# W0 transposed, from batch 1 on, read from DRAM in each batch, two landing slots of two rows each, in place of the copy in SBUF

## What is computed

```
x1 = x  + x @ W0.T + b0 + coeff[b] * (x @ (2*mask[b] - 1))      # mask[b]: 1024 x 1024 int32, here all ones
x2 = x1 + x1 @ W1eff.T                                          # W1 quantized by group, plus a LoRA term
x3 = x2 + x2 @ W2.T + b2 + 2 * (x2 @ A2[tok2[b]]) @ B2[tok2[b]]
out = x3 + (x3 @ B3[tok3[b]].T) @ A3[tok3[b]].T
```

## Time and profile before

| what | value |
|---|---|
| median of 3 runs | 557.78 us (557.56 to 558.84) |
| the profiled execution | 557.65 us, span 555.6 us |
| TensorE matmul busy | 541.3 us, 97% of the span |
| VectorE, ScalarE, GpSimd busy | 398.2, 328.9, 157.8 us |
| DMA queue of SyncE | 78.71 MB, 51.8% of 16 engines' span |
| mask loads | 64 of 512 KB, median 4.5 us from issue to landing |
| merges (line 1078) | 64, 78.3 us, mean 1.234 us |

### The profile page before, as it was taken

How to read it: one execution, slowest core, us unless ns; L and a number is a source line. 1 busy time by engine, 2 the same in 40 slices (tenths; PEclk the granted TensorE clock), 3 DMA queues, 4 the chain that set the end, 5 groups by cost and what they waited for, 6 DMA issues and landing times.

```text
span 555.6 us, 8876 instructions
## 1 busy us (share of the span) xinstructions
PE 541.3 (97%) x2892; PEld 464.6 (84%) x2892; DVE 398.2 (72%) x622; ACT 328.9 (59%) x622; POOL 157.8 (28%) x170
## 2 busy tenths in 40 slices
PE   5999999999999999999999999999999999999997
PEld 4988888888888788888888888888888888888886
DVE  5998898988956859666765875866687487586631
ACT  3877766776655846564564664656557466564620
POOL 2769778987714040021012002102100300210200
PEclk9999999999999999999999999999999999999999
DMA  8766042733577982574475366256447635634202
GB/s 230 246 88 143 21 145 62 248 97 113 120 192 231 314 204 97 170 186 69 149 221 113 132 187 156 63 170 197 76 151 226 114 119 163 174 73 151 76 0 76
DMA packets 138120, 80.07 MB, mean 144 GB/s; under 512 B 95664, under 2 KB 111024, under 8 KB 138096
## 3 DMA queue, kind: packets, MB, share of 16 engines
q1 hardware_dynamic: 137520, 78.71, 51.8%
q0 software_dynamic: 288, 1.05, 0.5%
q10 hardware_dynamic: 288, 0.01, 0.0%
HBM read 65.59 MB, written 14.16 MB: 144 GB/s over the span
## 4 chain that ended last, share of the span: by engine, by line
PE 84%; DVE 8%; ACT 4%; DMA 3%; issue 1%; POOL 0%; DVEq 0%; ACTq 0%; SPq 0%; POOLq 0%
PE bank L1432 19%; PE bank L1468 10%; PE bank L1469 10%; PE bank L1470 10%; PE bank L1439 10%; PE bank L1306 5%; PE bank L1308 5%; PE bank L1307 5%; PE bank L1478 3%; PE bank L1216 2%; PE bank L1485 1%; DVE merged_ring L1078 1%; DVE w_lo L984 1%; DMA mask_ring<-in_mask_Bx4096x_ik 1%; ACT bank L574 1%; PE bank L1230 1%
## 5 line engine op out<-in xcount | busy, mean ns | idle before, releaser
L1432 PE MATMUL bank<-x_t_pair,m_hi 128*128 128x512 f32 x512 | 128.4, 393 | 1.8 <-ACT m_hi L740 1.6
L740 ACT CAST m_hi<-merged_ring 128x512 fp32r<-128x512 f32 x128 | 73.0, 618 | 66.1 <-PE bank L1439 34.1
L1432 PEld LDWEIGHTS bank<-x_t_pair,m_hi 128*128 128x128 f32 x512 | 92.5, 189 | 19.5 <-ACT m_hi L740 2.6
L1084 DVE TENSOR_TENSOR m_lo<-merged_ring,m_hi 128x512 fp32r<-128x512 f32 x128 | 82.4, 689 | 30.7 <-ACT m_hi L740 30.6
L1468 PE MATMUL bank<-P_hi,x_t_pair 128*128 128x512 f32 x256 | 99.7, 389 | 0.0
L1469 PE MATMUL bank<-P_lo,x_t_pair 128*128 128x512 f32 x256 | 99.7, 389 | 0.0
L1470 PE MATMUL bank<-P_hi,x_t_pair 128*128 128x512 f32 x256 | 99.6, 389 | 0.0
L530 POOL TENSOR_TENSOR x_t_pair<-x_sum,x_t_pair 128x256 fp32r<-128x256 f32 x32 | 24.8, 801 | 260.5 <-ACT x_t_pair L781 260.5
L1078 DVE TENSOR_TENSOR merged_ring<-merged_ring,w_t 128x1024 f32<-128x1024 f32 x64 | 78.3, 1234 | 21.6 <-ACT merged_ring L730 20.6
L730 ACT ACTIVATE merged_ring<-mask_ring,batch_now 128x1024 f32<-128x1024 int32 x64 | 77.9, 1241 | 23.1 <-DMA mask_ring<-in_mask_Bx4096x_ik 22.3
L1439 PEld LDWEIGHTS bank<-x_t_pair,m_lo 128*128 128x128 f32 x512 | 69.9, 190 | 5.0
(11 more groups left out here) (152 smaller groups left out, 869.6 us busy)
## 6 DMA issues: line engine op xcount, KB each, us to landing
mask_ring<-in_mask_Bx4096x_ik SPq DMA_DIRECT2D x64, 512.0 KB, 4.5
out<-out_staged SPq DMA_DIRECT2D x32, 256.0 KB, 2.1
w_nat<-in_L_cond_W SPq DMA_DIRECT2D x14, 512.0 KB, 5.1
x_t_squares<-in_x SPq DMA_DIRECT2D x56, 128.0 KB, 2.7
w_raw<-in_L_cond_weight SPq DMA_DIRECT2D x16, 256.0 KB, 4.5
g_batch<-g_dram SPq DMA_DIRECT2D x32, 128.0 KB, 4.5
w0t_dram<-w_out SPq DMA_DIRECT2D x14, 256.0 KB, 2.7
w_t<-w0t_dram SPq DMA_DIRECT2D x6, 512.0 KB, 5.2
```

The costliest lines, as they stand in the source:

```text
L740: nc.scalar.copy(Mh[:, n % MR], ring_f[:, k % MR, h * HALF:(h + 1) * HALF]).then_inc(s["h_set"], 1)
L1084: nc.vector.tensor_tensor(Ml[:, n % MR], ring_f[:, k % MR, h * HALF:(h + 1) * HALF], Mh[:, n % MR].bitcast(F32), ALU.subtract).then_inc(s[ ...
L1432: mm(bank[L0_BANK[HT * h + j]][:, :], Mh[:, n % MR, j * P:(j + 1) * P], xThl[:, :, :, k + i, :], start=(k + i == 0), stop=False, skip_grou ...
```

## The change

From batch 1 on merge j no longer reads `w0t` in SBUF. It reads a landing place `land` [128, 2, 1024] float32 (two slots of 4 KB in each partition, at the start of region z3, where the raw chunks of W1, `W1h_late` and `w7` lay), into which SyncE loads part j from `w0t_dram`, slot j mod 2, when merge j-2 is done. Batch 0 still reads `w0t`, which stays allocated. Row 7 is therefore stored to DRAM once, from `w7`. The merge waits for its slot. SyncE's order in a batch becomes: loads 2 and 3, masks 4 and 5, loads 4 and 5, the stores, loads 6 and 7, masks 6 and 7, tables, mask 0 of the next batch, its load 0, its mask 1, its load 1, its masks 2 and 3, x, the stores.

```diff
+    land = at("w0_landing", [P, 2, D], F32, reg_z3)
...
+        w0_land = [s["w0_land0"], s["w0_land1"]]
...
+            def load_w0(b, j):
+
+                sp.wait_ge(s["v_set"], KT * b + j - 1)
+                sp.dma_start(land[:, j % 2].rearrange("p (i n) -> p i n", i=2),
+                             w0t_dram[part_rows(j), :, part_cols(j)].rearrange("k p n -> p k n")).then_inc(w0_land[j % 2], 16)
+
+            def next_mask(b, k):
+                done = 2 * KT * b + 2 * k + 2
+                if k < MR:
+                    sp.wait_ge(s["m_ready"], done)
+                    load_mask(b, k + MR)
                 else:
-                    sp.wait_ge(s["out_done"], 4 * b)
+                    sp.wait_ge(s["m_ready"], done)
+                    load_mask(b + 1, k - MR)
...
+            def load_next(b, last):
                 if not last:
-                    for k in range(MR):
-                        sp.wait_ge(s["m_ready"], 2 * KT * b + 2 * (k + MR) + 2)
-                        load_mask(b + 1, k)
+                    for k in range(MR, KT):
+                        next_mask(b, k)
+                        if k < MR + 2:
+                            load_w0(b + 1, k - MR)
 
                     sp.wait_ge(s["m_used"], 2 * KT * (b + 1))
                     load_x(b + 1)
-                if first:
-
-                    sp.wait_ge(s["xt_later"], 2)
-                    sp.dma_start(b2all[:, :], row(b2).broadcast_to([P, D])).then_inc(s["b2row_in"], 16)
+
+            def first_batch():
+                for k in range(MR):
+                    load_w0t(k + MR)
+                    next_mask(0, k)
+
+                sp.wait_ge(s["w7_eyed"], 1)
+                sp.dma_start(w0t_dram[KT - 1], w7[:, :, :].rearrange("p t c -> p (t c)")).then_inc(s["w7_stored"], 16)
+                sp.wait_ge(s["p_used"], KT * G)
+                load_tables(0)
+
+                sp.wait_ge(s["w7_stored"], 16)
+                sp.wait_ge(s["w7_placed"], 2)
+                load_next(0, False)
+                sp.wait_ge(s["xt_later"], 2)
+                sp.dma_start(b2all[:, :], row(b2).broadcast_to([P, D])).then_inc(s["b2row_in"], 16)
+                store(0, 0)
+
+            def batch(b, last=False):
+                load_w0(b, 2)
+                load_w0(b, 3)
+                next_mask(b, 0)
+                next_mask(b, 1)
+                load_w0(b, 4)
+                load_w0(b, 5)
+                store(b - 1, 1)
+                load_w0(b, 6)
+                load_w0(b, 7)
+                next_mask(b, 2)
+                next_mask(b, 3)
+                sp.wait_ge(s["out_done"], 4 * b)
+                load_tables(b)
+                load_next(b, last)
                 store(b, 0)
...
-                nc.vector.tensor_tensor(part, part, w0t[:, part_rows(j), part_cols(j)], ALU.add).then_inc(s["v_set"], 1)
+                if first:
+                    row = w0t[:, part_rows(j), part_cols(j)]
+                else:
+                    dve.wait_ge(w0_land[j % 2], 64 * (b - 1) + 16 * (j // 2 + 1))
+                    row = land[:, j % 2].rearrange("p (i n) -> p i n", i=2)
+                nc.vector.tensor_tensor(part, part, row, ALU.add).then_inc(s["v_set"], 1)
```

More of the change, by code:

```diff
@@ L203, in cond_resid_chain @@
             delta_done raw_used w2_eyed eff_plain normed terms pool_added scaled inner_set inner_up mid_set mid_up eff_set w1_hi_set w1_ready
-            p_used p_done p_hi p_ready w0_tr w0_evac w0_eyed w7_in w7_turned w7_eyed w7_placed dve_step pool_step act_step
+            p_used p_done p_hi p_ready w0_tr w0_evac w0_eyed w7_in w7_turned w7_eyed w7_placed w7_stored w0_land0 w0_land1 dve_step pool_step act_step
             s_set v_set h_set m_ready m_used l0_done x1_part x1_sum x1_hi x1_ready0 x1_ready1 x_turned xt_hi xt_first xt_later xt_ready u_done u_part u_summed u_hi u_ready c_ready
@@ L398, in store, with load_tables @@
                     sp.dma_start(dst, staged[:, h]).then_inc(out_stored[h], 16)
[L400 to L403, removed]
-                    if first:
[L406 to L410, removed]
-                else:
-                    sp.wait_ge(s["out_done"], 4 * b)
+            def load_w0(b, j):
[7 more added lines that the diff above has]
+                    load_mask(b, k + MR)
+                else:
+                    sp.wait_ge(s["m_ready"], done)
+                    load_mask(b + 1, k - MR)
+            def load_tables(b):
                 for part, rows in ((0, 0), (0, 32), (1, 64), (0, 96)):
@@ L415, in batch @@
                     sp.dma_start(Gs[rows:rows + 32, :].bitcast(F32), src).then_inc(s["g_in"], 16)
+            def load_next(b, last):
                 if not last:
-                    for k in range(MR):
-                        sp.wait_ge(s["m_ready"], 2 * KT * b + 2 * (k + MR) + 2)
-                        load_mask(b + 1, k)
+                    for k in range(MR, KT):
+                        next_mask(b, k)
+                        if k < MR + 2:
+                            load_w0(b + 1, k - MR)
                     sp.wait_ge(s["m_used"], 2 * KT * (b + 1))
                     load_x(b + 1)
-                if first:
-                    sp.wait_ge(s["xt_later"], 2)
-                    sp.dma_start(b2all[:, :], row(b2).broadcast_to([P, D])).then_inc(s["b2row_in"], 16)
+            def first_batch():
[27 more added lines that the diff above has]
+                load_next(b, last)
                 store(b, 0)
-            batch(0, first=True)
+            first_batch()
             with sp.Fori(1, NB - 1) as b:
```

## The result

| | before | after |
|---|---|---|
| median | 558.31 us (557.56 to 559.66, 4 runs) | 584.35 us (581.89 to 587.63, 4 runs) |
| profiled execution, its span | 557.65, 555.6 us | 584.53, 582.5 us |
| TensorE matmul busy | 541.3 us, 97% | 547.8 us, 94% |
| MB moved | 78.71 in SyncE's queue | 108.60 in it |

The ratio is 1.0467, with a 95% interval of 1.0411 to 1.0524: 26 us, 4.7% slower. The forecast was 563.4 us in a range of 557.4 to 574.

A forecast was written before the change was run, and what follows sets the result against it. TensorE, busy 97% of the span, was taken to bound the kernel. Late masks and casts in layer 0 cost 0.8 us in each of seven batches, 5.6 us on 557.78, giving 563.4 us, range 557.4 to 574.

The forecast's parts named there:

- the first link: Layer 0, loads 2 and 3: merges 2 and 3 wait for their landing, merge 3 ending 1.4 us late.
- the price of a load: SyncE's queue: each added 512 KB load takes 1.45 us of DMA time, ends 1.31 and 1.67 us.
- the second link: Layer 0, loads 4 and 5: merge 4 at 320.5 instead of 317.71, 1.25 us to spare, nothing lost.
- the third: Layer 0, loads 6 and 7 ahead of mask 6: it lands at 330.05, about 0.1 us lost at pair 5.
- The term for pair 7: Layer 0, cast of pair 7 comes late for TensorE: 0.6 to 0.7 us more per batch.
- No bound by volume: DMA engines over a whole batch: eight loads raise their share from 0.53 to about 0.78, so volume doesn't bound.
- rival B: Deep queue: landings in the mixed queue run late, 2 to 3.5 us lost per batch, 572 to 582 us; chance 0.20.
- The stalls forecast are shorter; no price: TensorE's granted clock: stays at the 2.4 GHz level through the forecast stalls, priced at zero.
- A: Covered: mask 6 lands before about 329.3, the cast of pair 7 is in time, not slower, 557.8 us; chance 0.33.
- C: Faster: a later mask load relieves a crowded spell in batch 0, could give 1 us there; chance 0.02.
- D: Change's text differs from what it does: landing lies at w1, not x's squares; no time, no chance given.
- the likeliest case: The forecast itself: layer 0 loses 0.3 to 1.8 us per batch, 563.4 us, own range 560 to 570; chance 0.45.

The follow-up runs named there:

- experiment 2: Changed kernel with all waits kept, but each load moves 16 of 128 partitions (64 KB) and merges read w0t in SBUF: 557.42 us, ratio 1.0007.
- volume_only: Changed kernel with the same loads, but no merge waits for one and merges read w0t in SBUF; SyncE waits for a slot's previous load: 571.48 us, ratio 1.0267.
- Experiment 7: Changed kernel with four landing slots, loads issued four merges ahead, and the next batch's loads 2 and 3 behind x: 559.68 us, ratio 1.0052.
- four_slots_x_first: Changed kernel with four landing slots instead of two and the next batch's loads 2 and 3 issued behind x: 559.68 us, ratio 1.0052.
- rows_4kb: Changed kernel with W0 transposed stored part by part in DRAM, so a load reads 128 runs of 4 KB, not 256 of 2 KB: 576.79 us, ratio 1.0374.
- no_tables: Changed kernel without the four table loads of batches 1 to 7, which use batch 0's adapter tables: 580.96 us, ratio 1.0437.

## Why the prediction was wrong

**Right.** The mechanism was the forecast one. Merges 2 and 3 wait for their landing, signs 6 for mask 6, TensorE for the casts of pair 5 and then 7, and the main product doesn't grow. Shifted by the 9.89 us by which batch 3 begins later, the forecast times of the first link hold to 0.1 us: load 2 issued at 310.7 (measured 310.92), merge 2 at 314.7 (314.81), merge 3 at 316.1 (316.22). Waits in SyncE's and VectorE's programs cost nothing themselves (experiment 2). A load's place in SBUF, and VectorE's operation on it, had no price (1.222 us a merge, 1.234 before).

**Right by luck.** The DMA share over the whole batch was to rise from 0.53 to "about 0.78" and was measured as 0.77. But the batch had grown from 46.83 to 51.51 us (327.96 to 379.47): the engines' time went from 24.8 to 39.7 us, 1.9 us for each of the eight loads where the forecast had 1.45. Two errors cancel in the share.

**The step that failed: the price of a load, and what lands behind it.** The prediction had mask 6 land at 330.05; shifted, it landed at 333.22. It was issued 1.0 us later than forecast and took 2.1 us longer. "I take 1.45 us" came from rates of a full queue in batch 0. Layer 0 of batch 3 held 0.57 x 22.33 = 12.7 us of DMA time for 4.02 MB before and 0.88 x 27.00 = 23.8 us for 6.86 MB after: 11.0 us for 2.84 MB, 5.4 loads, or 2.04 us each (time of packets under way, and so the price in a queue as full as this one). In volume_only the same working gives 2.0 us ((0.92 x 24.66 - 12.7) us for 2.6 MB). All of these lie above the upper end of 1.67 us, and the prediction's own sign of being wrong, a load under 320 GB/s, came true (2.04 us are 257 GB/s). With it goes the rule "in a queue it lands one load's time behind the one ahead": the second link came 0.9 us late (merge 4 at 321.42 shifted, for 320.5), and the third 2.1 us more, since mask 6 took 7.3 us from issue to landing where the forecast had 5.15 (324.9 to 330.05). Signs 6 were forecast at 330.1 and came at 333.25. Most of these 3.2 us were there two places ahead of mask 6: load 6 was forecast to land at 327.15, 4.1 us after its issue, and took 5.84 us, to 329.72 shifted. The prediction had said that the times past 330 move by 5 to 7 times a change of the load's time; 0.4 to 0.6 us too little per load made 0.1 us lost at pair 5 into 1.2 to 3.0. That is 15.0 of the 27 us for a forecast 0.7. The term for pair 7 was sized rightly (0.6 to 0.7, measured 0.7), though it was paid in five batches and not in seven.

**Why it was chosen so.** "No bound by volume" was read from the mean share of a whole batch. The loads don't stand evenly in it: 5.4 of the eight fall into layer 0, where the share was to go not to 0.78 but to 0.92 with the forecast's own price ((12.7 + 5.4 x 1.45) / 22.33). That number was there to be had from the earlier trace rows, and it speaks for rival B, whose argument, 1 us more on each link, is what happened. Its price, "2 to 3.5 us per batch", lay just under the measured 3.86 (27.0 / 7). "Against": that the queue of a later batch is not full was wrong for the stretch that matters, where the engines are at 1.01 while mask 6 is under way.

The rule beside rival B is that of the Trainium skill (DMA: Bandwidth & Descriptors, Latency and other measured facts): the latency of HBM grows from 0.2 to 2 us at high load. The runs agree in direction: mask 6 took 7.3 us with the engines at 1.01 and 3.9 us with them at 0.59. The difference of 3.4 us is more than the rule's, and in this kernel it comes and goes with what stands ahead in the queue; how much of it is latency and how much the packets ahead, no run separates.

**A term that was missing.** The start of a batch: "merges 2 and 3 1.4 us late" was seen, but not that an output sum stands behind them on VectorE and gives layer 0 its bank (4.2 us, two batches above all). The working followed VectorE's order from merge 4 on and not between merge 3 and it.

**A term priced at zero.** "The stalls forecast are shorter; no price" for the clock. With stalls of 2.88 us at pair 5 (batch 3) and 2.41 us (batch 1) the granted clock fell to 0.50, and the matmuls behind cost 1.65 us more each time, 3.3 us in all. The row that it rested on, had a TensorE idle for 1.25 us. The premise was right, the stalls weren't.

**The rivals.** A wanted mask 6 to land before 329.3; it landed at 333.2. Experiment 7 is the nearest to A: there the cover holds. B was the nearest to the measurement, and its 582 lies 2 us below it. C and D didn't occur. The 560 to 570 of the likeliest case stopped short by more than the clock and the bank together.

**Open.** The loss at pair 5 alternates: 2.5 to 3.0 us in odd batches, 1.2 to 1.6 in even ones, with load 6 landing after 5.8 to 6.0 and 3.8 to 4.2 us. In batch 3 load 6 (issued at 333.77) meets a slow stretch, 121 GB/s from 335 to 337, in batch 4 the same stretch (386.5 to 388.5) moves 263 GB/s; what makes every other batch slow there is not settled. Nor is why four_slots_x_first still pays 0.5%, though the trace says where: 0.6 us before batch 1, and 0.6, 0.5 and 0.3 us in layer 0 of batches 1, 3 and 7. And one change was not tried: the cast of pair 5 needs merge 5, which ended at 334.45, and the place of pair 3 in the ring, which TensorE was done with at about 339, but not mask 6. It waits for mask 6 only because ScalarE's written order puts signs 6 ahead of it.

## What to carry to other kernels

Price added transfers in the stretch of the queue where they stand, with the rate and the landing times of that stretch, and never by the mean share of a whole period. A mean share that comes out as forecast proves nothing where the time under it has grown too. In one queue fed in program order ask of every transfer what stands ahead of it: the one that is wanted next goes first, those that only refill a slot go behind, and a wider distance between issue and use (two more slots and an exchange of places: 584 to 560 us with the same bytes) does more than a faster load. An exchange moves the loss to whatever now stands behind, here x, so follow all that the queue carries through a full period.

## What the runs showed of the hardware that was not expected

A window of two microseconds in batch 3 with the new loads in flight, and one over the tables and a mask:

```profile
335.00:337.00 2.00, 2.00 (x14) 1.81 (x13) 2.00 (x5) 0.97 (x2) 0.00 (x0) 1.00 0.90 121
...
342.00:347.00 5.00, 2.12 (x8) 1.70 (x8) 2.50 (x4) 3.86 (x8) 0.00 (x0) 0.91 1.03 177
```

The engines are busy for 0.90 of the first at 121 GB/s, and for all of the second at 177 GB/s, where batch 0 moved 399 GB/s at a share of 1.05. The share says that packets are under way, not what they move. Between the two windows, with load 7 and masks 6 and 7 in the queue, the changed kernel moves 410 GB/s too:

```profile
339.50:341.50 2.00, 2.00 (x13) 1.71 (x12) 0.00 (x0) 0.00 (x0) 0.00 (x0) 1.00 1.06 410
```

The tables (128 KB and 32 partitions each) were issued from 337.66 on and can't be what slows the first window; a store of 256 KB (333.31 to 335.81), loads 6 and 7 and, from 335.83 on, mask 6 were under way there. What makes the rate so low was not taken apart.

A 512 KB load took from 3.8 us, with little ahead of it, to 9.0 us (mask 7 of batch 3, behind loads 6 and 7 and mask 6) and 9.4 us (mask 0 of batch 4, behind mask 7 and the tables) from issue to landing. Runs of 4 KB in DRAM in place of 2 KB brought 7.5 us in all, with the same bytes and the same number of loads.

TensorE's granted clock fell to the 1.2 GHz level after idle stretches of 2.41 and 2.88 us at pair 5, and stayed at the 2.4 GHz level after ones of 2.32 (batch 5) and 2.53 us (batch 7). In other runs it fell after 1.91 us (rows_4kb, batch 1) and stayed after 2.41 us (no_tables, batch 3). So the length of the idle time alone doesn't decide; what else does was not tried.
